# A scan kernel: W's third chunk behind the stack on another queue, the diagonals one place later, seven slots for C

## The chip, the cores and the metric

The kernel runs on one core of one Trainium2 chip. The metric is the device time of one execution in microseconds (us). The engines are PE (TensorE, matmuls), DVE (VectorE), ACT (ScalarE), POOL (GpSimd) and SP (SyncE, which here only issues transfers). SP and ACT each issue their transfers on a queue of their own; the profile calls SP's queue q1 and ACT's q10. An instruction waits for counters (semaphores) that other engines or landing transfers raise, and everything behind it on its engine waits too.

## What is computed

The input is x, 32 batches of 64 steps with 1024 channels. Two things follow each other, each added to its input:

```python
# first: adapted linear layer, then a selective scan
xc = x @ W + lora(x)                          # one adapter per batch
dt_in, B, C = split(xc @ x_proj_w.T)          # 32, 16, 16 columns
dt = softplus(dt_in @ dt_proj_w.T + dt_proj_b)
dA = exp(dt[..., None] * A)                   # 16 states per channel
dBx = dt[..., None] * B[:, :, None, :] * xc[..., None]
h = dA_t * h + dBx_t                          # for each step t
y = sum_over_states(h * C_t) + D * xc
x1 = x + y
# second: linear layer with adapter, then four experts of rank 16, two chosen by a router
x2 = x1 @ W2.T + bias2 + lora2(x1)
out = x1 + sum_over_chosen_experts(gate_e * ((x2 @ A_e.T) @ B_e.T)) * 4
```

## The kernel before

The 32 batches are worked in 8 **groups** of 4 batches (256 tokens). A group has 8 **steps** j, one for each 128 channels, and a step has 4 **units** `un`: half of the 16 states (8) for half of the tokens, so a unit is a tile of 128 partitions by 1024 elements. A place in the program is written (j, un); (0, 0) is a group's first unit and (7, 3) its last. There are 256 units in all, and each runs through the engines like this:

- PE makes `dBx` (`b_times_dtx`, L1191, its matmuls recorded at L1051): it multiplies a `stacked` tile, which holds dt*x, by `Bd`, the diagonal spread of B.
- ACT makes `dA`, 4 exponentials to a unit (L613). DVE runs the scan into `h` (L1012). There are two buffers each of `dBx` and `h`.
- POOL multiplies `h` by `Cb`, the unit's C spread over the partitions, into `hC` (L579, four buffers).
- PE sums `hC` over the states three units later (`sum_states`, L1224 and L1229), and DVE adds the residual (L820).

Everything else (the linear layers of the next groups, the second half of the layer for the group before) is cut into **jobs** and filled in between the units by the tables `JOBS`, `FIRST`, `SIXTH` and `FINAL`. A job's PE part runs at its unit; ACT and DVE take its result at the same unit or the next. The order on each engine is therefore fixed when the program is written.

What the change touches:

- **dt*x goes through memory.** POOL makes `dtx` (L559) for a step, PE transposes it (job `stack`), ACT and DVE split it into `HL` (L638, L907), SP stores `HL` to `dtx_scratch` (`put_dtx`, L421) and, one unit later and after that store has landed, loads it back in three transfers into `stacked` (`stack_dtx`, L428). Jobs stack 8 and stack 9 at (7, 0) and (7, 2) belong to steps 0 and 1 of the next group.
- **W** is kept in `W_scratch` in 8 chunks of 1 MB. `Wst` has two slots. Chunk i + 2 is loaded (`load_W`, L349) when job `cond` i has used its slot; ACT does this one unit after the job has ended. Cond 0 of the group after next ends at (7, 2), so chunk 2 is issued by ACT at (7, 3).
- **Diagonals.** `b_diagonals` (L830) makes a quarter of `Bd` for the next group, once the old quarter was used for the last time. `DIAGONALS` places the four behind the scans of (6, 3), (7, 1), (7, 3) and, in the next group, (0, 1). A group's `dBx` of unit un needs quarter un.
- **C.** Job Bst at (6, 2) is followed by `put_c` (L406, four small stores to `c_scratch`). `spread_c` (L416) loads one unit's C, 512 KB, into slot un of `Cb`. It has four slots, and each is free once POOL has made the last `hC` of step 7 from it. So SP issues the loads at (7, 1), (7, 2), (7, 3) and, in the next group, (0, 1).

Of the kernel before, what the change touches and what calls it, by code (L numbers as in the profile page):

```python
# [4 lines left out]
P = 128  # L5
# [6 lines left out]
K = D // P  # L12
# [3 lines left out]
HS = R // 2  # L16
# [5 lines left out]
ROWS = 3 * Q  # L22
NDA, NH, NHC, NDT = 2, 2, 4, 4
PARTS = ((0, 0), (0, 1), (1, 0))
# [99 lines left out]
ADAPTERS = {(1, 2): LORA2_B, (3, 0): 0, (4, 0): 1, (5, 2): 2}  # L124
DIAGONALS = {(0, 1): 3, (6, 3): 0, (7, 1): 1, (7, 3): 2}


def layer_kernel(nc, x, ids1, ids2, W, loraA, loraB, A_log, Dw, xproj_w, dtproj_w, dtproj_b,
# [6 lines left out]
    with ctx:  # L135
# [40 lines left out]
        Bd = sb("Bd", [P, NQ, R, Q], fr)  # L176
        Cb = sb("Cb", [P, UNITS, UNIT])
        x1 = sb("x1", [P, 2, TT, D])
# [27 lines left out]
        def xT_of(part, i):  # L206
# [4 lines left out]
               x1T[:, 4:8, :].rearrange("p k t -> p (k t)"), x1[:, 0, 0, :], x1[:, 0, 1, :], hC[:, 1, :], hC[:, 2, :], hC[:, 3, :]]  # L211
        Wraw = [Cb[:, :, :].rearrange("p u c -> p (u c)").rearrange("p (k o) -> p k o", k=K // 2),
                dA[:, :, :].rearrange("p h c -> p (h c)").rearrange("p (k o) -> p k o", k=K // 2)]
# [119 lines left out]

        def times_C(un):
            return (hC[:, un % NHC, :].rearrange("p (n b t) -> p b n t", n=HS, b=2),
                    h[:, un % NH, :].rearrange("p (b n t) -> p b n t", n=HS, b=2),
                    Cb[:, un, :].rearrange("p (b n t) -> p b n t", n=HS, b=2))

# [25 lines left out]
        def _(sp_e):  # L364
# [46 lines left out]
            def spread_c(G, un):  # L411
                if un == 0:
                    wait(sp_e, cscr_out, 64 * G + 64)
                wait(sp_e, hC_made, UNITS * K * G - UNITS + un + 1)
                src = c_scratch[G]
                sp_e.dma_start(Cb[:, un, :], src[un:un + 1, :].to_broadcast([P, UNIT])).then_inc(C_in[un], 16)  # L416

# [58 lines left out]
            def body(G, par):  # L476
                last = G == GROUPS - 1
                first = G == 0
                two_more = G + 2 < GROUPS
                for j in range(K):  # L480
                    t = K * G + j
                    for un in range(UNITS):
                        if un == 0:
                            load_xres(G, j, t)
                        if (j, un) == (0, 1) and not first:
                            spread_c(G, UNITS - 1)
                        which = ADAPTERS.get((j, un))
                        if which == LORA2_B:
                            load_lora2_b(G)
                        elif which == LORA2:  # L490
                            load_lora2(G)
                        elif which == LORA_A and two_more:
                            load_lora_a(G + 2)
                        elif which == LORA_B and two_more:
                            load_lora_b(G + 2)
                        for name, i, g, gpar, psum in ended_before(G, par, j, un):
                            if name == "stack":
                                stack_dtx(g, i)
                        for name, i, g, gpar, psum in ended_at(G, par, j, un):
                            if name == "stack":  # L500
                                put_dtx(g, i)
                        for name, i, g, gpar, psum in ended_at(G, par, j, un):
                            if name == "Bst":
                                put_c(g)
                            if name == "out":
                                store(g, i)
                        if j == K - 1 and un >= 1 and not last:

                            spread_c(G + 1, un - 1)

# [11 lines left out]
        def _(pool):  # L522
# [44 lines left out]
            def body(G, par):  # L567
                first, final = (G == g for g in (0, GROUPS - 1))
                for j in range(K):
                    for un in range(UNITS):  # L570
# [7 lines left out]
                        ns = slice(0, HS // 2 if s + 1 == UNITS * K * GROUPS else HS)  # L578
                        pool.tensor_tensor(*(x[:, :, ns, :] for x in times_C(un)), ALU.mult).then_inc(hC_made, 1)  # L579
                        if (j, un) in DTX and not (final and DTX[j, un] >= K):  # L580
# [6 lines left out]
        def _(act):  # L587
# [178 lines left out]
            def body(G, par):  # L766
                last = G == GROUPS - 1
                for j in range(K):
                    for un in range(UNITS):
# [11 lines left out]
                        for name, i, g, gpar, psum in ended_before(G, par, j, un):  # L781
                            if name in LATE_ON_ACT:
                                job(name, i, g, psum)
                            if name == "xT" and (1 < g if i < 2 else g + 1 < GROUPS):
                                load_x(act, g + i // 2, (i + 2) % 4)
                            if name == "cond" and i + 2 < K:
                                load_W(act, g, i + 2)
                            elif name == "cond" and g + 1 < GROUPS:
                                load_W(act, g + 1, i + 2 - K)
# [20 lines left out]
        def _(dve):  # L810
# [218 lines left out]
            dve.wait_ge(C_in[UNITS - 1], 16 * GROUPS)  # L1029
            dve.tensor_tensor(*(x[:, :, HS // 2:, :] for x in times_C(UNITS - 1)), ALU.mult).then_inc(last_half, 1)  # L1030
            add_residual(G, G % 2, K - 1, K * GROUPS - 1)
# [330 lines left out]
```

## Time and profile before

| | |
|---|---|
| runs | 904.91 us median of 3 (897.29 to 908.58) |
| profiled execution | 902.84 us, of which 901.0 us are the span from first to last instruction |
| PE matmul | 808.5 us busy (90% of the span) |
| PE weight load | 772.3 us (86%) |
| DVE | 763.6 us (85%), of it 583.2 in 256 scans |
| POOL | 687.9 us (76%) |
| ACT | 641.2 us (71%) |
| DMA | 172 MB, mean 191 GB/s |

Two engines and their partners share the work almost evenly, so the shares alone do not say what a change in one place is worth. That is read from the stretch itself: how long it lasts in one group and in another, and who waits there for whom.

### The profile page before, as it was taken

The page shows a single profiled execution, that of the slowest core. Times are in us where ns is not written, and L with a number is a line of the kernel's source. Part 1 is how long each engine was busy: PE and PEld are TensorE (multiplying, and loading weights), DVE is VectorE, ACT ScalarE, POOL GpSimd, SP SyncE. Part 2 cuts the span into 40 slices and gives each one's busy share as a digit, 9 for nine tenths or more (in the row PEclk, how much of TensorE's full clock was granted, in tenths as well). Part 3 has the DMA queues.
Part 4 walks back from the last instruction along what each step waited for, and adds up shares of the span by engine and source line. Part 5 has one row for each costly group of instructions (what it writes and reads, how often), then busy time and mean ns, then how long its engine had stood idle before and what let it go on. Part 6 is the DMA issues. An engine that isn't in the chain of part 4 may idle for free.

```text
span 901.0 us, 18654 instructions
## 1 busy us (share of the span) xinstructions
PE 808.5 (90%) x6427; PEld 772.3 (86%) x6427; DVE 763.6 (85%) x688; ACT 641.2 (71%) x1489; POOL 687.9 (76%) x349
## 2 busy tenths in 40 slices
PE   5998999999997999899997998889998999679785
PEld 4988998899987998799986998889988999578684
DVE  3446789989997899988997888998999889999994
ACT  3656678778776877878784876778777876678760
POOL 2015778889877888889877887889878988799892
PEclk9996999999998999999998999999999999889999
DMA  9988687476567657485666556476573744153221
GB/s 240 384 333 285 185 260 230 144 220 189 194 170 231 196 171 239 136 271 158 202 203 202 192 150 235 136 252 200 192 225 138 238 153 158 54 181 102 83 70 47
DMA packets 103113, 172.24 MB, mean 191 GB/s; under 512 B 21865, under 2 KB 71657, under 8 KB 94830
## 3 DMA queue, kind: packets, MB, share of 16 engines
q1 hardware_dynamic: 85614, 94.12, 35.1%
q10 hardware_dynamic: 17408, 76.95, 24.8%
q8 instruction: 53, 0.87, 0.4%
q14 instruction: 38, 0.31, 0.1%
HBM read 137.33 MB, written 33.69 MB: 190 GB/s over the span
## 4 chain that ended last, share of the span: by engine, by line
PE 58%; DVE 11%; ACT 9%; POOL 8%; issue 7%; DMA 5%; SPq 1%; POOLq 0%; ACTq 0%; DVEq 0%
PE jb L1051 25%; PE yp L1224 15%; PE dBx L1051 8%; POOL hC L579 7%; DVE h L1012 6%; ACT dA L613 5%; PE jb L1055 4%; PE yp L1051 3%; DMA stacked<-dtx_scratch 2%; DVE Bd L830 1%; POOL dtx L559 1%; DMA dtx_scratch<-HL 1%; DMA x<-in_x 1%; PE yp L1055 1%; DVE HL L907 1%
## 5 line engine op out<-in xcount | busy, mean ns | idle before, releaser
L579 POOL TENSOR_TENSOR hC<-h,Cb 128x1024 f32<-128x1024 f32 (+1 forms) x256 | 634.6, 2482 | 142.3 <-DVE h L1012 127.6
L1012 DVE TENSOR_TENSOR_SCAN h<-dA,dBx 128x1024 f32<-128x1024 f32 x256 | 583.2, 2280 | 62.8 <-PE dBx L1051 54.0
L613 ACT ACTIVATE dA<-dt,negA 128x252 f32<-128x252 f32 x1024 | 430.1, 494 | 74.4 <-DVE h L1012 64.0
L1224 PE MATMUL yp<-ident,hC 128*128 128x128 f32 x2048 | 275.6, 279 | 25.2 <-DVE dt L814 13.8
L1224 PEld LDWEIGHTS yp<-ident,hC 128*128 128x128 f32 x2048 | 237.7, 144 | 29.9 <-POOL hC L579 19.1
L1051 PE MATMUL jb<-xT,Wst 128*128 128x256 f32 x1416 | 214.3, 294 | 4.0 <-DVE dt L814 4.0
L1051 PE MATMUL dBx<-Bd,stacked 96*128 96x256 f32 x1024 | 188.1, 307 | 18.0 <-DMA stacked<-dtx_scratch 9.1
L1051 PEld LDWEIGHTS jb<-xT,Wst 128*128 128x128 f32 x1416 | 183.8, 192 | 6.7 <-DVE dt L814 4.8
L1051 PEld LDWEIGHTS dBx<-Bd,stacked 96*128 96x128 f32 x1024 | 147.9, 197 | 24.3 <-issue 21.3
L559 POOL TENSOR_TENSOR dtx<-dt,u 128x256 f32<-128x256 f32 x64 | 52.4, 819 | 39.4 <-DVE dt L814 39.4
L648 ACT ACTIVATE u<-jb 128x512 f32<-128x512 f32 x31 | 18.5, 598 | 35.0 <-PE jb L1051 32.6
L830 DVE TENSOR_TENSOR Bd<-Bhl,diag 96x1024 fp32r<-96x1024 f32 x32 | 38.8, 1214 | 0.1
L1051 PE MATMUL jb<-low,GB 128*128 128x256 f32 x128 | 38.1, 379 | 0.0
L911 DVE TENSOR_TENSOR xT<-jb,xT 128x512 fp32r<-128x512 f32 x26 | 17.8, 685 | 22.8 <-ACT xT L642 22.6
L642 ACT ACTIVATE xT<-jb 128x512 fp32r<-128x512 f32 x26 | 15.5, 596 | 29.1 <-PE jb L1055 28.5
L1229 PE MATMUL yp<-ident,Du 128*128 128x128 f32 x128 | 35.0, 274 | 0.0
L1051 PE MATMUL jb<-G,x1T 128*128 128x132 f32 x256 | 33.7, 279 | 1.0 <-ACT x1T L640 0.7
L640 ACT ACTIVATE x1T<-jb 128x512 f32<-128x512 f32 x32 | 19.1, 596 | 21.6 <-PE jb L1055 21.1
L1051 PEld LDWEIGHTS jb<-G,x1T 128*128 128x128 f32 x256 | 30.8, 190 | 1.8 <-ACT x1T L640 0.9
L604 ACT ACTIVATE Du<-u,Dsb 128x256 f32<-128x256 f32 x64 | 31.6, 495 | 0.0
L1051 PE MATMUL jb<-u,xprojT 128*128 128x256 f32 x128 | 30.5, 381 | 0.7 <-ACT u L648 0.7
L820 DVE TENSOR_TENSOR x<-yp,xres 128x256 f32<-128x256 f32 x64 | 26.2, 409 | 2.5 <-PE yp L1229 2.5
(178 smaller groups left out, 720.5 us busy)
## 6 DMA issues: line engine op xcount, KB each, us to landing
Wst<-W_scratch ACTq DMA_DIRECT2D x54, 1024.0 KB, 5.9
stacked<-dtx_scratch SPq DMA_DIRECT2D x192, 128.0 KB, 2.7
dtx_scratch<-HL SPq DMA_DIRECT2D x64, 256.0 KB, 2.9
Cb<-c_scratch SPq DMA_DIRECT2D x32, 512.0 KB, 5.5
xres<-in_x SPq DMA_DIRECT2D x64, 128.0 KB, 3.8
out<-obuf SPq DMA_DIRECT2D x28, 256.0 KB, 4.0
xin<-in_x ACTq DMA_DIRECT2D x26, 256.0 KB, 4.8
GB<-in_L_cond_lora_B SPq DMA_DIRECT2D x64, 64.0 KB, 5.6
```

Source lines behind the costliest of these rows:

```text
L559: pool.tensor_tensor(dtx[:, i % 2, :], dt[:, i % NDT, :], u[:, i % K, :], ALU.mult).then_inc(dtx_made, 1)
L579: pool.tensor_tensor(*(x[:, :, ns, :] for x in times_C(un)), ALU.mult).then_inc(hC_made, 1)
L604: act.activation(Du[:, i % 4, :], u[:, i % K, :], ACT.Copy, scale=Dsb[:, i % K:i % K + 1]).then_inc(Du_made, 1)
L613: act.activation(dA[:, half % NDA, :].rearrange("p (b n t) -> p b n t", b=GB_, n=HS)[:, :, n, 1:STEPS], dt[:, j % NDT, :].rearrange("p (b ...
L640: act.activation(x1T[:, 2 * i:2 * i + 2, :].rearrange("p k t -> p (k t)"), psum[:, :], ACT.Copy).then_inc(taken[name], 1)
L820: dve.tensor_tensor(x1[:, par, :, P * j:P * (j + 1)], yp[j % 2][:, 0:T].rearrange("p (tt d) -> p tt d", tt=TT), xres[:, t % NXRES, :, :], ...
L830: dve.tensor_tensor(Bd[0:ROWS, NQ // 2 * p:NQ // 2 * (p + 1), HS * half:HS * (half + 1), :], Bhl[0:ROWS, NQ // 2 * p:NQ // 2 * (p + 1), HS ...
L1012: dve.tensor_tensor_scan(h[:, un % NH, :], dA[:, half % NDA, UNIT * p:UNIT * (p + 1)], dBx[un % 2][:, :], 0.0, ALU.mult, ALU.add).then_inc ...
L1051: return pe.matmul(o, lhsT, rhs, start=start, stop=stop, **kw)
L1055: return pe.matmul(o, in_, ident[first:first + n, first:first + n], is_transpose=True, start=True, stop=True)
L1224: last = pe.matmul(y, hC[:, un % NHC, P * n:P * (n + 1)], ident[:, :], is_transpose=True, start=un == 0 and n == 0, stop=False, skip_group ...
L1229: last = pe.matmul(y, Du[:, j % 4, P * p:P * (p + 1)], ident[:, :], is_transpose=True, start=False, stop=True, skip_group_check=True)
```

## The change

It has three parts, all around the border between two groups.

1. The load of W's chunk 2 for the group after next leaves ACT's queue. SP issues it, directly behind the store `put_dtx` of stack 9 at (7, 2).
2. The diagonals stand one place later: behind the scans of (7, 1), (7, 3), and of (0, 0) and (0, 1) in the next group.
3. `Cb` has seven slots, taken in turn. The first three loads of C for the next group are issued at the end of (6, 3), right behind the stores of `put_c`, and the fourth at the end of (7, 3). With seven slots, the first three find slots that were last used in the group before the present one; the fourth finds the slot of unit 0 of the present group.

```diff
-NDA, NH, NHC, NDT = 2, 2, 4, 4
+NDA, NH, NHC, NDT, NCB = 2, 2, 4, 4, 7
-DIAGONALS = {(0, 1): 3, (6, 3): 0, (7, 1): 1, (7, 3): 2}
+SPREAD = {(6, 3): (0, 1, 2), (7, 3): (3,)}
+DIAGONALS = {(0, 1): 3, (7, 1): 0, (7, 3): 1, (0, 0): 2}
-        Cb = sb("Cb", [P, UNITS, UNIT])
+        Cb = sb("Cb", [P, NCB, UNIT])
+        def C_slot(G, un):
+            return (UNITS * G + un) % NCB
             def spread_c(G, un):
                 if un == 0:
                     wait(sp_e, cscr_out, 64 * G + 64)
-                wait(sp_e, hC_made, UNITS * K * G - UNITS + un + 1)
+                s = UNITS * G + un - NCB
+                if s >= 0:
+                    sp_e.wait_ge(hC_made, UNITS * K * (s // UNITS + 1) - UNITS + s % UNITS + 1)
                 src = c_scratch[G]
-                sp_e.dma_start(Cb[:, un, :], src[un:un + 1, :].to_broadcast([P, UNIT])).then_inc(C_in[un], 16)
+                sp_e.dma_start(Cb[:, C_slot(G, un), :], src[un:un + 1, :].to_broadcast([P, UNIT])).then_inc(C_in[un], 16)
-                        if (j, un) == (0, 1) and not first:
-                            spread_c(G, UNITS - 1)
                             if name == "stack":
                                 put_dtx(g, i)
+                                if i == K + 1 and two_more:
+                                    load_W(sp_e, G + 2, 2)
-                        if j == K - 1 and un >= 1 and not last:
-                            spread_c(G + 1, un - 1)
+                        for ahead in SPREAD.get((j, un), ()) if not last else ():
+                            spread_c(G + 1, ahead)
                             if name == "cond" and i + 2 < K:
-                                load_W(act, g, i + 2)
+                                if (i, g) != (0, G + 2):
+                                    load_W(act, g, i + 2)
-    nc = _bacc.Bacc("TRN2", target_bir_lowering=False, num_devices=1, dynamic_dma_scratch_size=1024)
+    nc = _bacc.Bacc("TRN2", target_bir_lowering=False, num_devices=1, dynamic_dma_scratch_size=512)
```

On SP, this is the border from group 1 to group 2 before, from the stores of C at (6, 2) to C's last load at (0, 1). `dtx_scratch<-HL` is `put_dtx`, `stacked<-dtx_scratch` is `stack_dtx`:

```order
L406 DMA c_scratch<-BC_GA 8x2x64 x4
L398 DMA xres<-in_x 128x2x128
L421 DMA dtx_scratch<-HL 128x512
L428 DMA stacked<-dtx_scratch 32x4x256 x3
L416 DMA Cb<-c_scratch 128x1024
L421 DMA dtx_scratch<-HL 128x512
L416 DMA Cb<-c_scratch 128x1024
L428 DMA stacked<-dtx_scratch 32x4x256 x3
L416 DMA Cb<-c_scratch 128x1024
L398 DMA xres<-in_x 128x2x128
L416 DMA Cb<-c_scratch 128x1024
```

And the same border after the change:

```order
L410 DMA c_scratch<-BC_GA 8x2x64 x4
L422 DMA Cb<-c_scratch 128x1024 x3
L402 DMA xres<-in_x 128x2x128
L427 DMA dtx_scratch<-HL 128x512
L434 DMA stacked<-dtx_scratch 32x4x256 x3
L427 DMA dtx_scratch<-HL 128x512
L353 DMA Wst<-W_scratch 128x2048
L434 DMA stacked<-dtx_scratch 32x4x256 x3
L422 DMA Cb<-c_scratch 128x1024
L402 DMA xres<-in_x 128x2x128
```

Three loads of C moved ahead of the first store of dt*x, none stands between the two stacks any more, and the 1 MB of W stands between the second store and its loads.

On DVE, this is before, from the scan of (6, 3) to that of (0, 2); `h<-dA,dBx` is a scan, `Bd<-Bhl,diag` a diagonal, and `dt<-` the job dtz, whose result releases a PSUM bank to PE:

```order
L1012 SCALAR_TENSOR_TENSOR h<-dA,dBx 128x1024
L830 TENSOR_TENSOR Bd<-Bhl,diag 96x4x256
L814 SCALAR_TENSOR_TENSOR dt<-jb,dt 128x512
L1012 SCALAR_TENSOR_TENSOR h<-dA,dBx 128x1024
L915 TENSOR_TENSOR low<-yp,own_batch 128x256
...
L1012 SCALAR_TENSOR_TENSOR h<-dA,dBx 128x1024
L830 TENSOR_TENSOR Bd<-Bhl,diag 96x4x256
L1012 SCALAR_TENSOR_TENSOR h<-dA,dBx 128x1024 x2
L830 TENSOR_TENSOR Bd<-Bhl,diag 96x4x256
L1012 SCALAR_TENSOR_TENSOR h<-dA,dBx 128x1024
```

And after:

```order
L1020 SCALAR_TENSOR_TENSOR h<-dA,dBx 128x1024
L822 SCALAR_TENSOR_TENSOR dt<-jb,dt 128x512
L1020 SCALAR_TENSOR_TENSOR h<-dA,dBx 128x1024
L923 TENSOR_TENSOR low<-yp,own_batch 128x256
...
L1020 SCALAR_TENSOR_TENSOR h<-dA,dBx 128x1024
L838 TENSOR_TENSOR Bd<-Bhl,diag 96x4x256
L1020 SCALAR_TENSOR_TENSOR h<-dA,dBx 128x1024
L838 TENSOR_TENSOR Bd<-Bhl,diag 96x4x256
L1020 SCALAR_TENSOR_TENSOR h<-dA,dBx 128x1024
L838 TENSOR_TENSOR Bd<-Bhl,diag 96x4x256
L1020 SCALAR_TENSOR_TENSOR h<-dA,dBx 128x1024
```

The diagonal ahead of the dtz job is gone from (6, 3), and one more stands between the first two scans of the next group.

## Rows read from the trace of the kernel before

**Rows 1.** The page: busy time by engine, share of the span, instructions.

```profile
PE 808.5 (90%) x6427; PEld 772.3 (86%) x6427; DVE 763.6 (85%) x688; ACT 641.2 (71%) x1489; POOL 687.9 (76%) x349
```

**Rows 2.** Windows at borders: length; busy PE, PEld, DVE, ACT, POOL; PEclk, DMA share, GB/s.

```profile
164.40:192.94 28.54, 25.68 (x216) 24.66 (x215) 23.80 (x20) 19.57 (x46) 24.11 (x13) 1.00 0.65 208
266.04:296.67 30.63, 25.08 (x197) 24.16 (x197) 23.97 (x20) 17.56 (x42) 23.92 (x13) 0.89 0.59 195
371.28:397.44 26.16, 23.00 (x192) 22.05 (x193) 23.80 (x19) 17.87 (x42) 23.91 (x12) 1.00 0.66 224
472.04:503.72 31.68, 25.64 (x192) 24.73 (x193) 23.97 (x19) 17.57 (x42) 23.93 (x13) 0.89 0.58 188
579.92:606.10 26.18, 23.02 (x192) 22.08 (x193) 23.81 (x20) 17.90 (x42) 23.93 (x12) 1.00 0.67 221
```

**Rows 3.** Timeline of PE, borders 1-2 and 3-4: start, duration, [idle before <-releaser].

```profile
281.16 1.19 PE L1051 MATMUL dBx<-Bd,stacked 96*128 96x256 f32 x4 [3.60 <-DMA stacked<-dtx_scratch]
...
487.32 1.20 PE L1051 MATMUL dBx<-Bd,stacked 96*128 96x256 f32 x4 [3.76 <-DMA stacked<-dtx_scratch]
```

**Rows 4.** Timeline of SP's and ACT's queues (issue times), border 1-2.

```profile
273.02 1.26 SPq L428 DMA_DIRECT2D stacked<-dtx_scratch  x3
...
273.73 0.37 ACTq L349 DMA_DIRECT2D Wst<-W_scratch  x1
...
276.43 0.34 SPq L421 DMA_DIRECT2D dtx_scratch<-HL  x1
```

**Rows 5.** DMA issues at 273.85 to 274.1 (border 1-2): KB each, us to landing.

```profile
stacked<-dtx_scratch SPq DMA_DIRECT2D x1, 128.0 KB, 6.9
```

**Rows 6.** DMA issues at 377.3 to 378.9 (border 2-3).

```profile
stacked<-dtx_scratch SPq DMA_DIRECT2D x3, 128.0 KB, 2.6
```

**Rows 7.** Timeline of POOL behind borders 0-1, 2-3 and 4-5.

```profile
190.42 4.73 POOL L579 TENSOR_TENSOR hC<-h,Cb 128x1024 f32<-128x1024 f32 x2 [2.64 <-DVE h L1012]
...
398.01 4.74 POOL L579 TENSOR_TENSOR hC<-h,Cb 128x1024 f32<-128x1024 f32 x2 [1.06 <-DMA Cb<-c_scratch]
...
606.95 7.29 POOL L579 TENSOR_TENSOR hC<-h,Cb 128x1024 f32<-128x1024 f32 x3 [1.34 <-PE yp L1224]
```

**Rows 8.** Timeline of DVE: scans of (1, 1) behind borders 2-3 and 4-5.

```profile
400.54 2.29 DVE L1012 TENSOR_TENSOR_SCAN h<-dA,dBx 128x1024 f32<-128x1024 f32 x1 [0.81 <-POOL hC L579]
...
609.47 2.29 DVE L1012 TENSOR_TENSOR_SCAN h<-dA,dBx 128x1024 f32<-128x1024 f32 x1 [1.10 <-ACT dA L613]
```

**Rows 9.** Timeline of PE, border 2-3.

```profile
371.42 2.05 PE L1051 MATMUL jb<-xT,Wst 128*128 128x256 f32 x15 [1.16 <-DVE dt L814]
...
391.71 0.41 PE L1055 MATMUL yp<-ident,dtx 128*128 128x128 f32 x2 [0.87 <-POOL dtx L559]
...
392.32 1.67 PE L1051 MATMUL jb<-xT,Wst 128*128 128x256 f32 x12
```

**Rows 10.** Timeline of POOL and DVE, border 2-3.

```profile
369.73 3.29 POOL L579 TENSOR_TENSOR hC<-h,Cb 128x1024 f32<-128x1024 f32 x1 [1.05 <-DVE h L1012]
...
389.81 1.76 POOL L559 TENSOR_TENSOR dtx<-dt,u 128x256 f32<-128x256 f32 x1
...
393.86 0.73 POOL L559 TENSOR_TENSOR dtx<-dt,u 128x256 f32<-128x256 f32 x1
...
389.79 1.20 DVE L830 TENSOR_TENSOR Bd<-Bhl,diag 96x1024 fp32r<-96x1024 f32 x1
```

**Rows 11.** Timeline of SP, border 3-4: the stores of C.

```profile
466.06 1.40 SPq L406 DMA_DIRECT2D c_scratch<-BC_GA  x4
```

**Rows 12.** DMA issues: dt*x from 372 and at 276.45; W at 289.75; C at 789.3.

```profile
dtx_scratch<-HL SPq DMA_DIRECT2D x1, 256.0 KB, 2.0
...
dtx_scratch<-HL SPq DMA_DIRECT2D x1, 256.0 KB, 6.0
...
Wst<-W_scratch ACTq DMA_DIRECT2D x1, 1024.0 KB, 4.8
...
Cb<-c_scratch SPq DMA_DIRECT2D x1, 512.0 KB, 3.6
```

More of the change, by code:

```diff
@@ L211, in layer_kernel @@
                x1T[:, 4:8, :].rearrange("p k t -> p (k t)"), x1[:, 0, 0, :], x1[:, 0, 1, :], hC[:, 1, :], hC[:, 2, :], hC[:, 3, :]]
-        Wraw = [Cb[:, :, :].rearrange("p u c -> p (u c)").rearrange("p (k o) -> p k o", k=K // 2),
+        Wraw = [Cb[:, 0:UNITS, :].rearrange("p u c -> p (u c)").rearrange("p (k o) -> p k o", k=K // 2),
                 dA[:, :, :].rearrange("p h c -> p (h c)").rearrange("p (k o) -> p k o", k=K // 2)]
@@ L332, in set_bank, with times_C @@
             return dBx[i % 4 // 2][:, 512 * (i % 2):512 * (i % 2 + 1)]
-        def times_C(un):
+        def C_slot(G, un):
+            return (UNITS * G + un) % NCB
+        def times_C(G, un):
             return (hC[:, un % NHC, :].rearrange("p (n b t) -> p b n t", n=HS, b=2),
                     h[:, un % NH, :].rearrange("p (b n t) -> p b n t", n=HS, b=2),
-                    Cb[:, un, :].rearrange("p (b n t) -> p b n t", n=HS, b=2))
+                    Cb[:, C_slot(G, un), :].rearrange("p (b n t) -> p b n t", n=HS, b=2))
         def W_chunk(o):
@@ L578, in body @@
                         ns = slice(0, HS // 2 if s + 1 == UNITS * K * GROUPS else HS)
-                        pool.tensor_tensor(*(x[:, :, ns, :] for x in times_C(un)), ALU.mult).then_inc(hC_made, 1)
+                        pool.tensor_tensor(*(x[:, :, ns, :] for x in times_C(G, un)), ALU.mult).then_inc(hC_made, 1)
                         if (j, un) in DTX and not (final and DTX[j, un] >= K):
@@ L1029, in _ @@
             dve.wait_ge(C_in[UNITS - 1], 16 * GROUPS)
-            dve.tensor_tensor(*(x[:, :, HS // 2:, :] for x in times_C(UNITS - 1)), ALU.mult).then_inc(last_half, 1)
+            dve.tensor_tensor(*(x[:, :, HS // 2:, :] for x in times_C(G, UNITS - 1)), ALU.mult).then_inc(last_half, 1)
             add_residual(G, G % 2, K - 1, K * GROUPS - 1)
```

## The prediction

> **What bounds the kernel now.** I read the page's busy times first: PE 90%, DVE 85%, POOL 76% [rows 1]. With two engines that close, neither is "the" bound, so I split the span by stages. Over most of a group DVE has no gap or PE paces it evenly; those stretches the change leaves alone. The borders are where groups differ. From the scan of (7, 0) to that of the next (1, 0) the same 9 units take 28.54, 30.63, 26.16, 31.68 and 26.18 us at the first five borders, while DVE is busy for 23.8 to 24.0 us in each [rows 2]. The work is the same; the waits differ. So the undisturbed border costs 26.16 us, and the excess is what can be had.
>
> Next I asked who ends those waits. In the timeline of PE the two longest waits for a transfer, 3.60 and 3.76 us for the landing of `stacked`, are the first `dBx` of a group at borders 1-2 and 3-4 [rows 3], the two long windows [rows 2], and in those windows alone of the five the granted clock is 0.89, in the other three 1.00. At border 1-2 SP issues the three loads of the stack from 273.02 to 274.28, and ACT issues 1 MB of W at 273.73, ahead of the third [rows 4]. That third load takes 6.9 us to land [rows 5]; at border 2-3, where all three are out before W, they take 2.6 [rows 6]. It is a race: half a microsecond decides whether a 128 KB transfer gets caught beside 1 MB. The runs of before spread from 897.29 to 908.58, 11.3 us or about two such hits, which fits a race.
>
> The second leak is C. The loads of units 2 and 3 are issued late and lie beside another chunk of W. POOL's `hC` of units 2 or 3 waits 2.64, 1.06 and 1.34 us behind borders 0-1, 2-3 and 4-5 [rows 7]. The profile names three different releasers, but only the middle row names C's load. All three are the units whose C is loaded last, so I put the other two waits down to C's load as well; that is an inference.
>
> **W behind the store.** The 1 MB no longer runs beside stack 8: it is issued after put 9, 2.7 us or more later than now (276.43 against 273.73, [rows 4]), when stack 8's loads have landed. Six loads move, of groups 0 to 5. What it removes: the excess at border 1-2, 30.63 - 26.16 = 4.5 us, and at border 3-4, 31.68 - 26.16 = 5.5 us. Both are more than PE's wait, since PE also ran at the lower clock for a while afterwards and lost its lead. **Minus 10.0 us.**
>
> What it costs: SP waits for nothing new, since cond 0 has ended when put 9 is issued. Behind W in SP's queue stand the three loads of stack 9 and the fourth of C. W alone lands in 4.8 us [rows 12]. Issued right behind put 9, which goes out at 276.43 [rows 4], 10.4 us after the scan of (7, 0), it leaves at 10.8 and lands at about 16, and at 18 if it takes 7. The third `cond` of the next group needs it at 392.32, that is 21.0 us after 371.28 [rows 9, 2]. Stack 9 then lands by about 20 (2.6 more), and its first use is just before the scan of (1, 0), 26 us after. Both are hidden with 3 us to spare or more. If the cover were gone, each microsecond late would cost one at six borders. ACT loses an issue of 0.37 us [rows 4] where it has idle time: nothing.
>
> **C early.** All four loads land before (0, 0), or soon after it. The waits of [rows 7] go. At border 0-1 that is the excess 28.54 - 26.16 = 2.4 us. Behind 2-3 and 4-5 the hold-up shows only one unit later, outside the window: DVE idles 0.81 and 1.10 us before the scan of (1, 1) [rows 8]. The usual wait there is about 0.2, so I take 0.6 and 0.9. **Minus 3.9 us.**
>
> What it costs: three loads of C, 1.5 MB, now lie ahead of put 8 in the same queue. At border 3-4, the latest, the stores of C are issued from 466.06 to 467.46 [rows 11]. A store lands in 2.0 us when nothing is beside it [rows 12], and I allow up to 3, so C goes out at about 470.0. One load takes 3.6 us, and 1 MB takes 4.8 [rows 12], so each further 512 KB costs between 1.2 and 2.4; three land after 6.0 to 8.4 us, at 476 to 478.4. At border 1-2 the stack's loads go out 7.0 us after the scan of (7, 0) (273.02 - 266.04, [rows 4, 2]), and the store ahead of them takes 2 to 3, so put 8 goes out some 4 us after that scan: here at 476, or 475 if the border starts a microsecond earlier. If it lands with the last of C at 478.4, the stack's third load lands about 3.6 later, at 482. PE wants it at 487.32 - 3.76 = 483.6 [rows 3], minus the microsecond that the border may start earlier. So even the latest border just holds: I take nothing. The row against it is the store that took 6.0 us with W and C beside it [rows 12]: put 8 would land at 481, the stack at 484.6, and PE would wait 2 us there.
>
> Here the Trainium skill ("DMA: Bandwidth & Descriptors", section "Queues, rings and completion order") speaks against the change: within one queue each of the 16 DMA engines takes descriptors in ring order, whereas two queues are served in turn, packet by packet. Issued on SP, C stands wholly in front of put 8 instead of beside it. By that rule put 8 lands with or after the last C, at 478.4, as in the bound that I used; by the 6.0 us row it would be 481. The sum by the rule is the one above; by the row it would be some 2 us plus clock at one or two borders.
>
> **The diagonals.** DVE's work stays the same, 1.20 us for each [rows 10]. At (6, 3) the dtz job comes earlier by one of them. PE waits for exactly that job before cond 0, for 1.16 us at border 2-3 [rows 9], and POOL's `hC`, which takes 3.29 us beside a diagonal [rows 10] and about 2.4 without (4.73 for two, [rows 7]), releases `dtx` 8 sooner. Gain: 0.4 us (where PE gets there late) to 1.16, I take 0.9, what POOL saves. At (0, 0) the same comes back. POOL has no slack there: `hC` of (0, 0) is now slowed by 0.9, and `dtx` 2 behind it still meets the next diagonal (1.76 us against 0.73, [rows 10]), and PE already waits 0.87 us for it [rows 9]. Cost: 0.9. **Net 0**, from a gain of 0.5 to a loss of 0.7 at each of seven borders.
>
> **The sum.** Against the profiled execution's own 902.84 us: 902.84 - 10.0 - 3.9 + 0 = 888.9; I say **889**. The median of before, 904.91, is 2.07 us above the profiled execution, and both hold such hits in a random number. A kernel without the race should not vary with them, so I do not add the 2 us. Its range: 884 (diagonals gain 0.5 at each of seven borders, and a microsecond at the remaining ones) to 894 (diagonals cost 0.7 at each).
>
> **The rivals.**
>
> *Put 8 late behind C.* For it: the 6.0 us row and the ring order; against it: C is issued 4 us or more ahead, where in that row W and C were out only 2 to 3 us ahead. It would leave the stall at two borders, 4.5 to 5.5 us each with the clock: 889 + 10 = 899. Chance 0.18.
>
> *The change doesn't remove the waits' cost* (hidden anyway: the next limit, PE's own pace or DVE's, takes up what is freed). For it: PE 90% busy. Against it: borders 2-3 and 4-5 show in 26.16 and 26.18 us what the program does without the hit. It would give about 903. Chance 0.05.
>
> *W or stack 9 late in SP's queue.* Price: W landing 2 us after its need at six borders, 889 + 12 = 901. It decides from a landing 10.2 us after the issue, and 6.9 us [rows 5] is the longest that I have a row for, of a load beside W. Chance 0.04.
>
> *Slower: the idle time of PE at (0, 2).* The wait of 0.87 us [rows 9] becomes 1.8. If PE's granted clock then falls for a few us, as around the waits of 3.6 us (a mean of 0.89 in the window [rows 2]), each border loses the diagonal's 0.9 us and some 1.8 of clock, without the gain at (6, 3): 7 x 2.7 = 19, which gives 889 + 19 = 908. It decides from five borders at which the clock falls. Against it: waits of 1.16 us left the clock at 1.00 in the window of border 2-3. Chance 0.05.
>
> **How the numbers follow.** The first case has 0.68 (884 to 894). Its upper neighbours reach to 901. The range 884 to 901 leaves out the case of no effect, the slower one, and the tails, under 2 in 10. A measurement of this kernel tells about 2% from no change, 18 us; faster by that means below 886.8, which is the lower fifth of the first case or somewhat more: 0.22. Slower by 2% (above 923) no case reaches: 0.02. Within 2%: 0.76.
>
> **What would show it.** No wait of PE for `stacked` over 1 us before a group's first `dBx`; windows from (7, 0) to (1, 0) of 26 to 27 us at all seven borders, with a clock of 1.00; no `hC` waiting for `Cb`; C's loads and put 8 landing before stack 8's third load is 2.6 us from its need; the wait before cond 0 at (7, 0) near zero, and that before stack 2 at (0, 2) near 1.8. The prediction is wrong if PE still waits for stack 8 (put 8 landing 6 us after its issue), if the third cond waits for W, or if the borders are even but longer than 27 us, which would mean the diagonals.

## The result

| | before | after |
|---|---|---|
| median of 20 runs | 905.14 us (895.97 to 912.34) | 895.95 us (889.43 to 903.15) |
| ratio | | 0.9916, 95% interval 0.9889 to 0.9943 |
| profiled execution | 902.84 us | 897.03 us |

The change gains 0.8% by the ratio; between the two medians lie 9.2 us, which is 1.0%. The gain is real and less than 2%. The median of 895.95 lies inside the forecast's range of 884 to 901. The forecast's 889 meant 15.9 us, or 1.8%, against the median of 904.91 known then: 9.2 us are little more than half of it, and 0.8% is less than half.

The page of the profile after, busy times by engine, answers to [rows 1]; nothing of substance moved there.

```profile
PE 803.0 (90%) x6427; PEld 765.2 (85%) x6427; DVE 762.6 (85%) x688; ACT 642.0 (72%) x1489; POOL 690.4 (77%) x349
```

The windows from the scan of (7, 0) to the next (1, 0), in the changed kernel's trace, borders 0-1 to 6-7 (columns as in [rows 2]: length, busy times of PE, weight load, DVE, ACT and POOL, granted clock, DMA):

```profile
167.00:194.31 27.31, 23.12 (x193) 22.09 (x193) 24.89 (x21) 19.05 (x45) 25.25 (x13) 1.00 0.58 191
267.78:295.08 27.30, 23.08 (x193) 22.04 (x193) 24.88 (x20) 19.03 (x45) 25.19 (x13) 1.00 0.62 207
368.57:395.93 27.36, 23.52 (x197) 22.40 (x196) 24.91 (x20) 18.93 (x45) 25.32 (x13) 1.00 0.70 226
469.40:496.78 27.38, 23.37 (x195) 22.19 (x194) 24.93 (x21) 19.06 (x45) 25.28 (x13) 1.00 0.68 226
570.25:597.57 27.32, 23.08 (x193) 22.04 (x193) 24.90 (x20) 19.04 (x45) 25.29 (x13) 1.00 0.65 219
671.04:698.38 27.34, 23.10 (x193) 22.05 (x193) 24.90 (x21) 19.04 (x45) 25.24 (x13) 1.00 0.58 189
772.65:801.87 29.22, 20.20 (x122) 18.84 (x123) 24.69 (x20) 18.92 (x45) 25.94 (x13) 0.77 0.29 94
```

Six borders are alike to a tenth of a microsecond, with a granted clock of 1.00. The seventh, which leads into the last group, took 29.2 us, with a clock of 0.77. Each of the six is 1.1 us longer than the undisturbed 26.16 of [rows 2] because one diagonal more stands in this window (DVE is busy for 24.9 us, not 23.8) and one less stands just ahead of it. Groups 1 to 5 each take 100.8 us from first scan to first scan, which was the best group of before. So the waits at these borders are gone, as forecast. The execution is nevertheless 8.1 us above 889. The longest wait of PE for a transfer stands in the first group, far from any border (timeline of PE, SP's queue and ACT's queue, changed kernel):

```profile
101.06 0.72 PE L1059 MATMUL dBx<-Bd,stacked 96*128 96x256 f32 x4 [4.17 <-DMA stacked<-dtx_scratch]
...
93.26 1.28 SPq L434 DMA_DIRECT2D stacked<-dtx_scratch  x3
...
94.15 0.35 ACTq L353 DMA_DIRECT2D Wst<-W_scratch  x1
```

And the two transfers in flight at 94.13 to 94.45 (KB, us to landing):

```profile
Wst<-W_scratch ACTq DMA_DIRECT2D x1, 1024.0 KB, 6.4
stacked<-dtx_scratch SPq DMA_DIRECT2D x1, 128.0 KB, 6.7
```

This is the picture of [rows 4] and [rows 5] at another place: the third load of a stack goes out beside 1 MB of W and lands 6.7 us later. The change removed one place of the race, not the race. This one hit is about half of the 8.1 us; the section on the prediction divides up the rest.

### The profile page after: what moved, and what is told of

The parts are those of the page before. It is cut to its first block, busy times and chain, and to the rows that moved or that the text cites. A ratio compares the mean times of both kernels' runs of the same rounds, so it can differ in the third digit from the quotient of the medians.

```text
span 895.3 us, 18653 instructions
## 1 busy us (share of the span) xinstructions
PE 803.0 (90%) x6427; PEld 765.2 (85%) x6427; DVE 762.6 (85%) x688; ACT 642.0 (72%) x1489; POOL 690.4 (77%) x349
## 4 chain that ended last, share of the span: by engine, by line
PE 50%; POOL 14%; DVE 14%; issue 10%; ACT 6%; DMA 4%; SPq 1%; POOLq 0%; ACTq 0%; DVEq 0%
PE jb L1059 23%; PE yp L1232 14%; POOL hC L586 12%; DVE h L1020 9%; PE dBx L1059 7%; PE jb L1063 3%; ACT dA L620 3%; DMA dtx_scratch<-HL 2%; POOL dtx L566 2%; PE yp L1059 2%; DMA x<-in_x 1%; DVE dt L822 1%; PE yp L1063 1%; DMA stacked<-dtx_scratch 1%; PE yp L1237 1%
## 5 line engine op out<-in xcount | busy, mean ns | idle before, releaser
L1232 PE MATMUL yp<-ident,hC 128*128 128x128 f32 x2048 | 270.8, 276 | 25.7 <-DVE dt L822 14.3
L1232 PEld LDWEIGHTS yp<-ident,hC 128*128 128x128 f32 x2048 | 233.3, 142 | 30.4 <-POOL hC L586 19.8
L1059 PE MATMUL dBx<-Bd,stacked 96*128 96x256 f32 x1024 | 185.3, 303 | 14.8 <-DMA stacked<-dtx_scratch 5.0
L1059 PEld LDWEIGHTS dBx<-Bd,stacked 96*128 96x128 f32 x1024 | 145.3, 194 | 20.9 <-issue 17.7
L566 POOL TENSOR_TENSOR dtx<-dt,u 128x256 f32<-128x256 f32 x64 | 54.9, 859 | 39.3 <-DVE dt L822 39.3
L1059 PE MATMUL jb<-u,xprojT 128*128 128x256 f32 x128 | 30.5, 381 | 0.7 <-ACT u L655 0.7
L828 DVE TENSOR_TENSOR x<-yp,xres 128x256 f32<-128x256 f32 x64 | 26.2, 409 | 2.5 <-PE yp L1237 2.5
```

Of the source, the lines that this page charges most:

```text
L566: pool.tensor_tensor(dtx[:, i % 2, :], dt[:, i % NDT, :], u[:, i % K, :], ALU.mult).then_inc(dtx_made, 1)
L828: dve.tensor_tensor(x1[:, par, :, P * j:P * (j + 1)], yp[j % 2][:, 0:T].rearrange("p (tt d) -> p tt d", tt=TT), xres[:, t % NXRES, :, :], ...
L1059: return pe.matmul(o, lhsT, rhs, start=start, stop=stop, **kw)
L1232: last = pe.matmul(y, hC[:, un % NHC, P * n:P * (n + 1)], ident[:, :], is_transpose=True, start=un == 0 and n == 0, stop=False, skip_group ...
```

## The experiments

Theory A says that the time hangs on hits, a load of `stacked` beside a chunk of W, wherever they happen. The other theories say that PE's pace takes up what is freed (B), that a slow store alone makes the waits in group 4 (C), and that the early loads of C have a worth of their own (D). Before was run beside each set on the same chip; its medians there were 903.1, 906.34 and 907.67 us, so ratios are compared, not times, between sets.

### One part at a time

**W alone** (the two edits of `load_W`, nothing else):

```diff
+                                if i == K + 1 and two_more:
+                                    load_W(sp_e, G + 2, 2)
...
-                                load_W(act, g, i + 2)
+                                if (i, g) != (0, G + 2):
+                                    load_W(act, g, i + 2)
```

> The kernel before with one part of the change: W's chunk 2 issued by SP behind the second store, C and the diagonals as before. Theory A (the stall of stack 8 beside W is what the change removes; the rest is elsewhere): no wait of PE over 1 us for stacked before a group's first dBx at any border; waits of POOL for C's last loads shrink but stay (0 to 2 us at some borders); median about 898 to 900 us, that is 5 to 7 us below before. Theory B (what is freed is taken up by PE's own pace): windows from (7, 0) to (1, 0) of 28 us and more without any such wait, median 903 to 906.

Measured: median 894.32 us, ratio 0.9891 (0.9844 to 0.9938), so the part alone does all that the change does; the smaller scratch allocation in the diff's last line is not in this kernel, and so is not what gains. No border had a hit, and the seven windows were 26.2 to 26.9 us. POOL waited nowhere for C either. The reason is in SP's queue. With W ahead of it on ACT's queue, the store of stack 9 took 4.7 to 6.4 us at the first six borders of before, and SP holds the stack's loads, and C's last two behind them, until it has landed. With W behind it, it took 2.2 to 3.5 us. Border 1-2, before and then in this run:

```profile
276.43 0.34 SPq L421 DMA_DIRECT2D dtx_scratch<-HL  x1
282.63 1.27 SPq L428 DMA_DIRECT2D stacked<-dtx_scratch  x3
283.94 0.43 SPq L416 DMA_DIRECT2D Cb<-c_scratch  x1
...
275.81 0.34 SPq L421 DMA_DIRECT2D dtx_scratch<-HL  x1
278.45 1.36 SPq L428 DMA_DIRECT2D stacked<-dtx_scratch  x3
279.85 0.43 SPq L416 DMA_DIRECT2D Cb<-c_scratch  x1
```

So C's load of unit 2 went out 2.9 to 3.5 us earlier in a border than before, with no edit to it. The profiled execution, 900.59 us, still had a wait of 3.76 us for `stacked`, before (5, 0) of group 4. The median was below what either theory expected.

**C alone** (`NCB = 7`, `C_slot`, `SPREAD`; W and diagonals as before):

> The kernel before with one part of the change: seven slots and early loads of C, W on ACT's queue and the diagonals as before. Theory A: POOL waits nowhere for C (3.9 us less in the profiled execution of before), but stack 8 still meets W, at as many borders as before or more, since put 8 now stands behind C: two to four waits of 3.5 us and more before a group's first dBx; median 900 to 905. Theory B (C's lateness was not a cause of its own): 905, as before.

Measured: 906.65 us, ratio 1.0004 (0.9964 to 1.0045): nothing. The trace had 26.2 us at four of the first six borders and 29.3 at border 3-4, where the store of stack 8 took 3.0 us behind the loads of C and the third load of the stack then went out with W and took 5.6. That was the only long wait before a group's first `dBx`, 2.44 us, where theory A expected two to four of 3.5 us and more; the profile names a diagonal as its end. POOL waited nowhere for C, and the median still did not move. Why not, at borders that cost so little in this trace, is not shown.

**The diagonals alone** (`DIAGONALS` as after):

> The kernel before with one part of the change: the diagonals one place later. Theory A (they cancel at borders 0-1 to 5-6 and cost at 6-7, where the trace after shows a low clock and a window of 29.2 us against 26.7): units (6, 3) and (7, 0) together 0.9 us shorter, (0, 0) and (0, 1) together 0.9 us longer; the window of border 6-7 28.5 to 29.5 us; median 905 to 908. Theory B (they cancel everywhere, and the long window of border 6-7 is chance): window 6-7 below 27.8 us, median 905.

Measured: 906.63 us, ratio 1.0026 (0.9996 to 1.0057). Undisturbed borders were 27.3 us, with 0.9 us less ahead of them; border 6-7 was 28.0, between the values of the two theories. They cancel, or cost a microsecond or two; the interval does not say which.

**W and C, diagonals put back** (`DIAGONALS` as before in the changed kernel):

> The changed kernel with its diagonals put back: W and C moved, diagonals as before. Theory A: windows from (7, 0) to (1, 0) of 26.2 us at borders 0-1 to 5-6 and below 27 at 6-7; group lengths of 100.8 us; 2 to 2.5 us below the changed kernel, median 893 to 894. Theory B (diagonals cancel everywhere): 896, as the changed kernel.

Measured: 895.17 us, ratio 0.9929 (0.9890 to 0.9969), no different from the changed kernel. Its profiled execution took 888.43 us: six borders of 26.2 us, 28.1 at border 6-7, and no hit anywhere. The runs spread from 888.43 to 903.63. So 889 is what this kernel takes when nothing is hit, and most runs take longer. The last border is as long here, without the late diagonals, as with them alone (28.0); only the trace of the changed kernel above had 29.2.

### Making the hit certain

W's chunk 2 issued by SP directly ahead of stack 8's loads, in the kernel of the last experiment:

```diff
                             if name == "stack":
+                                if i == K and two_more:
+                                    load_W(sp_e, G + 2, 2)
                                 stack_dtx(g, i)
...
                                 put_dtx(g, i)
-                                if i == K + 1 and two_more:
-                                    load_W(sp_e, G + 2, 2)
```

> The changed kernel with the diagonals put back and W's chunk 2 issued by SP directly ahead of stack 8's loads, so that the hit happens at six borders in every run. Theory A (a hit costs 4.5 to 5.5 us with the clock, as in the profiled execution of before): windows of 30.5 to 32 us from (7, 0) to (1, 0) at borders 0-1 to 5-6, PE waiting 3 to 5 us for stacked at each; median 918 to 928. Theory B (PE's pace takes up part of it): windows of 28 us, 905.

Measured: 928.46 us median, ratio 1.0289 (1.0218 to 1.0360). The windows of borders 0-1 and 1-2, of its trace, and PE's wait in the first:

```profile
161.46:192.36 30.90, 25.05 (x192) 24.14 (x193) 23.98 (x19) 17.59 (x42) 23.94 (x13) 0.89 0.44 144
266.97:297.87 30.90, 25.28 (x192) 24.37 (x193) 23.98 (x19) 17.57 (x42) 23.95 (x13) 0.89 0.48 165
...
176.55 1.19 PE L1057 MATMUL dBx<-Bd,stacked 96*128 96x256 f32 x4 [3.59 <-DMA stacked<-dtx_scratch]
```

All six borders took 30.5 to 30.9 us, with the granted clock at 0.89. The price of one hit is therefore 4.3 to 4.7 us over 26.2, of which PE's wait is 3.4 to 3.7. The rest goes with the clock: the 192 matmuls of such a window kept PE busy for 24.6 to 25.3 us, against 23.0 in an undisturbed one. Theory B is out. The profiled execution was 921.12 us, and 888.43 + 6 x 4.5 = 915.4; two hits before (5, 0), of 3.9 us in group 2 and 1.2 in group 4, make most of the rest. The median lies above theory A's range, and by the ratios some 33 us above the kernel of the last experiment, 5.4 to a border; what takes more than the 4.3 to 4.7 of the trace is not shown.

### The second place

Stack 5 is loaded at (4, 1) to (4, 2), and ACT issues W's chunk 0 for the group after next right then. The windows from the scan of (4, 1) to that of (5, 2), groups 2 to 4, in a second trace of the changed kernel (899.33 us):

```profile
331.96:351.84 19.88, 17.02 (x121) 15.91 (x120) 15.22 (x15) 10.87 (x27) 13.98 (x7) 0.91 0.56 176
436.43:452.64 16.21, 15.21 (x121) 14.28 (x120) 15.14 (x14) 10.88 (x27) 13.97 (x7) 1.00 0.61 182
537.24:556.86 19.62, 15.44 (x121) 14.33 (x120) 15.22 (x14) 10.87 (x27) 13.94 (x7) 1.00 0.56 179
```

And the issues in group 4 of that trace:

```profile
541.13 1.28 SPq L434 DMA_DIRECT2D stacked<-dtx_scratch  x3
541.68 0.33 ACTq L353 DMA_DIRECT2D Wst<-W_scratch  x1
```

Undisturbed it is 16.2 us, so two hits cost 3.7 and 3.4. In group 4 this trace has the third load issued 0.3 us behind W, and it took 6.3 us. For that second trace I had written:

> The changed kernel once more, for a second trace. Theory A: no hit at any border; a hit before (5, 0) of group 4 or (2, 0) of group 0, or none, and the time follows: 889 to 892 without, 5 us more for each.

The median was 897.84 us over 8 runs, ratio 0.9888 (0.9852 to 0.9925). There was no hit at a border, and two before (5, 0), one of them in a group that the expectation had not named. The kernel before, traced once more, was to show the same two sources:

> The kernel before once more, for a second trace. Theory A: hits at other borders than in the first trace, one to three of them, and their windows from (7, 0) to (1, 0) of 30 to 32 us; undisturbed borders 26.2 us.

It took 908.52 us. Its windows at borders 1-2, 2-3 and 4-5, then the second place in group 4, and the same place in the first trace of before:

```profile
263.95:295.03 31.08, 25.87 (x192) 24.96 (x193) 23.98 (x20) 17.57 (x42) 23.96 (x13) 0.89 0.58 191
371.50:399.79 28.29, 25.22 (x210) 24.12 (x210) 23.80 (x19) 19.57 (x46) 24.18 (x13) 1.00 0.62 210
...
583.42:612.10 28.68, 25.48 (x211) 24.33 (x212) 23.80 (x19) 19.67 (x47) 24.18 (x13) 1.00 0.60 207
...
542.42:563.96 21.54, 17.04 (x121) 15.93 (x120) 15.25 (x14) 10.87 (x27) 13.94 (x7) 0.92 0.54 165
...
542.68:560.46 17.78, 15.45 (x121) 14.34 (x120) 15.22 (x14) 10.88 (x27) 13.91 (x7) 1.00 0.64 198
```

The stalls came at the same two borders, 1-2 and 3-4, not at others as expected; the store of stack 8 is slow there in both traces (2.9 and 3.3 to 3.4 us against 2.0). It is so in all thirteen traces, whatever the kernel: 2.3 to 3.0 us for group 2 and 3.0 to 3.7 for group 4, and 2.0 to 2.1 for groups 5, 6 and 7. With before's order of transfers (both its traces and that of the diagonals alone) these two borders were hit every time, so the hits there look fixed and not drawn by chance; what makes these stores slow is open. At borders 2-3 and 4-5 POOL waited for C. And the second place cost 21.5 - 16.2 = 5.3 us in this trace against 1.6 in the first (17.78 us). In the trace on which the forecast was made, that place was nearly quiet. In the nine traces of kernels that load this chunk as before did, the windows of this place are longer than 16.2 us by 0, 0, 1.6, 5.1, 5.3, 6.6, 6.8, 7.1 and 7.4 us in all.

**W's chunk 0 behind the store of stack 6**, the same trick there, in the changed kernel with the diagonals put back:

```diff
+                                if i == 6 and two_more:
+                                    load_W(sp_e, G + 2, 0)
...
                             elif name == "cond" and g + 1 < GROUPS:
-                                load_W(act, g + 1, i + 2 - K)
+                                if i != 6:
+                                    load_W(act, g + 1, i + 2 - K)
```

> The changed kernel with the diagonals put back, and with W's chunk 0 for the group after next issued by SP behind the store of stack 6 at (4, 2) instead of by ACT at (4, 3). Theory A (the same race stands at (4, 1) to (4, 3), where stack 5's loads meet this chunk, and takes 6 to 9 us in group 4 in four of six profiles so far): no wait of PE for stacked before (5, 0) in any group, group 4 at 100.8 us, median about 891 to 893, spread narrower than 12 us. Theory C (the long waits in group 4 come from something else, a slow store at a fixed time, and need no W beside them): group 4 still 105 us and more now and then, median 895.

Measured: 891.04 us median, ratio 0.9847 (0.9802 to 0.9893), and six runs within 889.63 to 892.77. The expectation overstates what stood in the six profiles then at hand: by the windows it was 6.6 to 7.4 us in three of them, and 1.6 in a fourth. The trace holds the test of theory C. The store of stack 5 in group 4 (first row), then its loads and W:

```profile
dtx_scratch<-HL SPq DMA_DIRECT2D x1, 256.0 KB, 3.9
...
536.01 1.28 SPq L434 DMA_DIRECT2D stacked<-dtx_scratch  x3
537.59 0.34 SPq L427 DMA_DIRECT2D dtx_scratch<-HL  x1
537.98 0.43 SPq L353 DMA_DIRECT2D Wst<-W_scratch  x1
...
531.81:548.60 16.79, 15.70 (x123) 14.48 (x121) 15.06 (x15) 11.42 (x29) 14.26 (x7) 1.00 0.73 209
```

The store is as slow as in the traces with a hit, yet the window is 16.79 us. Another trace with this edit (the last experiment below) has a store of 4.0 us there and a window of 16.5. A slow store does little harm without W beside the loads behind it. Theory C is out; what makes the store slow in group 4 was not found.

**The first group.** W's chunk 1 for group 1 also moved, behind the store of stack 2:

> The kernel of the run before it, and W's chunk 1 for group 1 issued behind the store of stack 2 in the first group instead of ahead of it, 1 MB of the 2 that now stand before that store. Theory A: the store of stack 2 lands in 3 us or less after W's chunk 0, stack 2's loads are out before ACT issues W's chunk 2, no wait of PE for stacked before (2, 0) of group 0; first group 104 to 106 us; median 888 to 890, lowest run about 887. Theory C: no change against the run before it.

Measured: 890.77 us, ratio 0.9848 (0.9802 to 0.9895). No further gain, and the first group took 108.3 us, not 104 to 106; the store of stack 2 took 4.6 us, not 3. The hit at 94 us stands in one of the thirteen traces only. Whether this edit would prevent it, six runs do not tell.

### What C and the diagonals are worth once W is out of the way

**W twice, nothing else** (before, with both chunks behind their stores, four slots for C):

> The kernel before with nothing but the two loads of W moved to SP: chunk 2 behind the store of stack 9, chunk 0 behind the store of stack 6; four slots for C and the diagonals as before. Theory A (the waits for C were made by the hits and by W beside C; the seven slots add nothing): POOL waits nowhere over 0.4 us for the C of units 0 to 2, median 890 to 892, as with the seven slots. Theory D (C's early loads are worth some 3.9 us of their own, as forecast): 894 to 895.

Measured: 892.60 us, ratio 0.9850 (0.9807 to 0.9893). The median lies between the two expectations, 1.6 us above the kernel with seven slots, which the intervals do not separate. Theory A's statement on POOL was wrong: its timeline behind border 1-2 shows the waits again:

```profile
287.31 2.40 POOL L583 TENSOR_TENSOR hC<-h,Cb 128x1024 f32<-128x1024 f32 x1 [1.37 <-DMA Cb<-c_scratch]
...
292.77 4.73 POOL L583 TENSOR_TENSOR hC<-h,Cb 128x1024 f32<-128x1024 f32 x2 [2.37 <-PE yp L1230]
```

The second row's wait is C's too, though the profile names another releaser: `hC` starts 0.16 us after that load has landed, as in every row that the profile puts down to C. That border took 29.7 us, the others 26.2 to 28.1, and POOL waited for C behind borders 3-4 and 5-6 as well. So late C is a cause of its own. By the medians it is worth some 1.6 us, with intervals that allow none, and not 3.9.

**The changed kernel with the second place mended**, late diagonals kept:

> The changed kernel as it is, its late diagonals too, with W's chunk 0 moved behind the store of stack 6. Theory A (the diagonals cancel at six borders and cost 1 to 2.5 us at the last): median 891.5 to 893.5, windows of 27.3 us with (6, 3) and (7, 0) 0.9 us shorter, and 29 us at border 6-7. Theory B (they cancel everywhere): 891, as with the diagonals put back.

Measured: 892.22 us, ratio 0.9845 (0.9803 to 0.9888), with 27.3 us at four of the first six borders and 28.0 at border 6-7, like the kernels without late diagonals (27.9 and 28.1). Between cancelling and a cost of a microsecond or so the runs do not decide. The 2.5 us more at the last border, 29.2 against 26.7, were in one trace of the changed kernel and not in its second, where that window was 27.3.

## Why the prediction was right or wrong

- **W behind the store, minus 10.0.** The mechanism holds: the clock, PE's wait and the window of a forced hit, 30.5 to 30.9 us, are those of [rows 2] and [rows 3], and the part alone gives the whole gain. Its size as a term, 4.5 and 5.5 for the two hits, is close to the forced 4.3 to 4.7.
- **C early, minus 3.9.** This term failed. The waits were C's, the two that the profile gives to others too: the loads of units 2 and 3 in question were issued at 182.45 and 598.50 us and took 7.8 and 8.3 us, and the `hC` of [rows 7] start at 190.42 and 606.95, 0.16 us after each landing.

```profile
L416 SPq DMA_DIRECT2D Cb<-c_scratch x1: 430/430/430, 182.4 to 182.4; - x1
DMA to landing us min/median/max: 7.8/7.8/7.8
...
L416 SPq DMA_DIRECT2D Cb<-c_scratch x1: 470/470/470, 598.5 to 598.5; - x1
DMA to landing us min/median/max: 8.3/8.3/8.3
```

  But a wait of POOL is not lost time as long as PE has work. The trace of before, from the scan of (1, 0) to that of (3, 0), behind border 0-1 and behind the undisturbed border 2-3:

```profile
192.94:214.62 21.68, 21.39 (x190) 20.88 (x190) 20.09 (x14) 16.99 (x40) 20.39 (x11) 1.00 0.64 191
397.44:420.91 23.47, 23.47 (x209) 23.07 (x208) 20.15 (x15) 18.64 (x45) 20.61 (x11) 1.00 0.63 189
```

  PE is busy for the whole of that stretch, so PE sets its length. In the long window at border 0-1 PE had gone on, with 25.7 us of work and 216 matmul records against 23.0 and 192 [rows 2], and the next two steps were 1.8 us shorter for it. Of the 2.4 us that I took, 0.6 were lost. Behind borders 2-3 and 4-5, where I took 0.6 and 0.9, nothing was: from (7, 0) to (3, 0) both took 49.63 us. So 3.9 us were 0.6 in that trace. The windows of a hit show no such work ahead (197 and 193), and their loss stays. The other check agrees: W alone had no wait for C in its trace, since the store of stack 9 lands sooner, C alone gave 1.0004, and with W moved twice the seven slots are worth 1.6 us between medians.
- **The diagonals, net 0.** As forecast, term by term. The timeline of DVE after, at border 2-3, shows the scans of (6, 3) and (7, 0), and those of (0, 0) and (0, 1):

```profile
365.79 2.28 DVE L1020 TENSOR_TENSOR_SCAN h<-dA,dBx 128x1024 f32<-128x1024 f32 x1
...
368.57 2.28 DVE L1020 TENSOR_TENSOR_SCAN h<-dA,dBx 128x1024 f32<-128x1024 f32 x1
...
382.68 2.27 DVE L1020 TENSOR_TENSOR_SCAN h<-dA,dBx 128x1024 f32<-128x1024 f32 x1
...
386.06 2.27 DVE L1020 TENSOR_TENSOR_SCAN h<-dA,dBx 128x1024 f32<-128x1024 f32 x1
```

  From (6, 3) to (7, 0) it is 2.78 us where it was 3.91, and from (0, 0) to (0, 1) 3.38 where it was 2.46. The units (6, 3) and (7, 0) together are 0.9 us shorter, (0, 0) and (0, 1) together 0.9 longer. PE's wait ahead of cond 0, 1.16 us in [rows 9], is gone, and its wait ahead of stack 2 is 1.8 us at four of the first six borders (0.8 and 1.4 at the others), as expected.
- **Put 8 behind C.** The verdict held, the times of the bound did not. At border 3-4 the three loads of C took 6.9 us in all, inside the 6.0 to 8.4, but the stack landed 11.6 us after the scan of (7, 0), not 10. At border 2-3 the store took 4.0 us, the longest; the stack landed 0.79 us after PE was ready for it, and the scan of (0, 0) waited for nothing. The store never took the 6.0 us of the rival. At all seven borders it landed after the last of the three loads of C.

```profile
381.15 0.71 PE L1059 MATMUL dBx<-Bd,stacked 96*128 96x256 f32 x4 [0.79 <-DMA stacked<-dtx_scratch]
```

- **W and stack 9 in SP's queue.** W landed 5.1 to 7.1 us after its issue, stack 9's loads by 19.7 us after the scan of (7, 0); nobody waited.
- **The steps that failed.** One is the term for C, 3.9 us for what was 0.6. The other is in the sum: "A kernel without the race should not vary with them, so I do not add the 2 us", and before it "those stretches the change leaves alone". I took one execution, subtracted its excess at the borders, and called the rest a floor. But the rest varied too. The spread of the runs, which I read as the two hits at the borders, was not theirs: those stand in both traces of before, and the changed kernel, without them, spread by 13.7 us over 20 runs. With the second place mended as well, four kernels spread by 2.7 to 6.6 us over six runs each, and their ratios are 0.9845 to 0.9850, where the four medians with only the first place mended gave 0.9888 to 0.9929. So that place is worth some 4 to 7 us of the median, and I had no term for it. The list of waits of before held the clue:

```profile
PE dBx L1051 <- DMA stacked<-dtx_scratch: 9.1, 4, 3.8
```

  These are four waits, 9.1 us in all, and the two that I used make 7.4. I did not ask where the others stood.
- **The two profiled executions, part by part.** The forecast took 13.9 us off 902.84; 897.03 is 5.8 below it. The first six borders, each from the scan of (6, 3) to that of the next (3, 0), before and then after; the first number is their length together:

```profile
sum 332.60, PE 305.75 PEld 297.18 DVE 287.39 ACT 241.50 POOL 283.85; mean PE 50.96 PEld 49.53 DVE 47.90 ACT 40.25 POOL 47.31
sum 323.34, PE 298.09 PEld 288.88 DVE 286.82 ACT 242.16 POOL 284.98; mean PE 49.68 PEld 48.15 DVE 47.80 ACT 40.36 POOL 47.50
```

  That is 9.3 us less, not 13.9. The stretches between them took 2.2 less, of which the quiet second place is 1.6. Up to the (6, 3) of the first group it was 3.7 us more, with the hit at 94 us, and from the (6, 3) of group 6 to the end 2.0 more. That 889 is so close to an execution without any hit (888.43 was profiled, 889.43 was the lowest of 20 runs of the changed kernel) is luck: the term for C took off 3.3 us too much, and about as much that an undisturbed execution is also spared, 1.6 us at the second place and 2.9 in the first group less 1.2 at the end, I had not taken off.
- **The chances.** Within 2% had 0.76, and it came so. The likeliest case got its range of 884 to 894 from terms of the borders alone, and the median lies above it, for a reason that none of the rivals names.

## What to carry to other kernels

When a stall turns out to be a race between two transfers, look for every place in the program where the same two kinds of transfer meet, and look at the spread of the runs: a fix at one place takes out the hits at that place, and the median keeps the rest. A meeting costs only where somebody is about to need the small transfer: the loads of stack 3 met a chunk of W in groups 1 to 6 of every trace, mostly landed after 5 to 6.5 us, and PE waited for none of them. Moving the large transfer behind the small one's store, at both places, gave 0.9845 to 0.9850 where one place gave 0.9888 to 0.9929. To forecast a median from one trace, sum what varies, not only what the change touches. And before an excess in a window is booked as a gain, look at the stretch behind it: if the pacing engine worked ahead in the long window, it gives the time back.

## What the runs showed of the hardware

Over the thirteen traces there are 210 loads of 128 KB that SP issued up to 1.1 us behind 1 MB of W on ACT's queue. They took 5.2 to 7.8 us to land, about as long as the 1 MB itself, where one takes 2.6 alone. Of 219 issued 0.45 to 1.5 us ahead of such a chunk, 209 took 2.3 to 3.6 us, and the longest took 7.0. In between, up to 0.45 us ahead, 76 loads took anything from 2.3 to 6.9: the third load of the hit at 94 us was issued 0.04 us ahead and took 6.7. So no distance found here makes the small load safe for certain.

The store of stack 9, 256 KB, took 4.7 to 6.6 us with W issued 2.7 us ahead of it on the other queue and a load of C on its own, in the two traces of before and in that of the diagonals alone. With W issued behind it, it took 2.1 to 2.7 us, and 3.4 and 3.5 at two borders.

One hit that holds PE for 3.4 to 3.7 us costs 4.3 to 4.7. The granted clock of the 31 us around it averages 0.89, and at border 1-2 of before it was 0.51, the lower of its two levels (1.2 GHz), from 277.90 to 284.80 us.
